# Kept rows turned by VectorE in 32x32 blocks, with the first step's h placed inside tile 6's choice

## The reference

```python
x = x + xattn(layernorm(x), ctx)          # 32 heads, 1601 keys of width 256, 8 kv heads
z = layernorm(x)
s = silu(z @ w_gate.T)                    # 1024 tokens x I = 2752
idx = top_k(-abs(s), k=I // 2)            # per token: the half of s that is smallest
s = s.at[idx].set(0)                      # is set to zero: 1376 values are kept
x = x + (s * (z @ w_up.T)) @ w_down.T
z = layernorm(x)                          # router: top 2 of 8 experts, each of rank 16
x = x + mixture(z)                        # h = z A, weighted, times B, times 8/R
```

## Time and profile before

| | |
|---|---|
| median of 3 runs | 1407.67 us (1404.67 to 1409.79) |
| profiled execution, its own time | 1406.26 us |
| its span in the trace | 1404.3 us |
| PE busy over the span | 1357.7 us (97%) |
| DVE, POOL, ACT busy | 989.0, 932.7, 740.8 us |
| DVE, ACT, POOL share | 70%, 53%, 66% |
| q1 (SP's and ACT's DMAs) | 193.68 MB, 89312 packets, 39.9% of 16 engines |

### The profile page before, as it was taken

How to read it: one execution, slowest core, us unless ns; L and a number is a source line. 1 busy time by engine, 2 the same in 40 slices (tenths; PEclk the granted TensorE clock), 3 DMA queues, 4 the chain that set the end, 5 groups by cost and what they waited for, 6 DMA issues and landing times.

```text
span 1404.3 us, 30491 instructions
## 1 busy us (share of the span) xinstructions
PE 1357.7 (97%) x12711; PEld 1007.6 (72%) x12711; DVE 989.0 (70%) x1324; ACT 740.8 (53%) x950; POOL 932.7 (66%) x627
## 2 busy tenths in 40 slices
PE   4999999999999999899999999999998999999996
PEld 3555555555555555599999998888876787887874
DVE  6888888888888888870000899999999323245655
ACT  6788888888888888742324634334241111111211
POOL 0799888888888988823344332323323899999892
PEclk9899999999999999999999999999999999999999
DMA  9023333233323230023436347557664876866552
GB/s 359 27 101 105 134 108 111 95 112 100 113 98 119 102 116 31 17 78 129 170 134 281 124 150 275 175 185 241 211 227 154 298 255 203 261 209 180 167 175 96
DMA packets 111469, 218.62 MB, mean 156 GB/s; under 512 B 8336, under 2 KB 84000, under 8 KB 106336
## 3 DMA queue, kind: packets, MB, share of 16 engines
q1 hardware_dynamic: 89312, 193.68, 39.9%
q10 hardware_dynamic: 22016, 22.96, 5.2%
HBM read 174.67 MB, written 41.94 MB: 154 GB/s over the span
## 4 chain that ended last, share of the span: by engine, by line
PE 76%; DVE 19%; DMA 1%; issue 1%; ACT 1%; SPq 0%; POOL 0%; POOLq 0%; DVEq 0%; ACTq 0%
PE fast_psum L1960 17%; PE fast_psum L2047 16%; PE fast_psum L2108 16%; PE fast_psum L1978 15%; PE fast_psum L1997 6%; DVE fast_below L1427 5%; DVE fast_near L1464 2%; DVE fast_near L1491 1%; PE fast_psum L2004 1%; DVE fast_top L1470 1%; PE fast_psum L2083 1%; DVE fast_sx L1497 1%; DMA fast_mag<-s 1%; PE fast_psum L2159 1%; PE fast_psum L1983 1%
## 5 line engine op out<-in xcount | busy, mean ns | idle before, releaser
L1357 DVE TENSOR_TENSOR fast_masked<-fast_psum,fast_mask_t 128x1024 f32<-128x1024 f32 (+1 forms) x416 | 488.4, 1219 | 72.2 <-PE fast_psum L1960 70.0
L1208 POOL TENSOR_TENSOR fast_pair<-fast_probs 128x1024 f32<-128x1024 f32 x192 | 457.1, 2384 | 96.3 <-PE fast_psum L1997 47.7
L1707 ACT ACTIVATE fast_probs<-fast_masked 128x1024 f32<-128x1024 f32 (+1 forms) x416 | 438.0, 1058 | 68.8 <-DVE fast_masked L1357 53.6
L1960 PE MATMUL fast_psum<-fast_qT,fast_kraw 32*128 32x256 f32 (+1 forms) x3328 | 247.1, 403 | 6.8 <-ACT fast_qT L1654 3.2
L1978 PE MATMUL fast_psum<-fast_probs,fast_vraw 128*32 128x256 f32 (+1 forms) x3328 | 226.5, 386 | 0.8 <-ACT fast_probs L1707 0.8
L1960 PEld LDWEIGHTS fast_psum<-fast_qT,fast_kraw 32*128 32x128 f32 (+1 forms) x3328 | 153.7, 182 | 93.3 <-DVE fast_masked L1357 53.9
L1268 POOL TENSOR_TENSOR fast_d_lo<-fast_d_raw,fast_d_hi 128x256 fp32r<-128x256 f32 x252 | 190.8, 787 | 5.0
L1241 POOL TENSOR_TENSOR fast_g_lo<-fast_g_raw,fast_g_hi 128x1408 fp32r<-128x1408 f32 x28 | 89.9, 3237 | 140.4 <-ACT fast_g_hi L1768 118.3
L2047 PE MATMUL fast_psum<-fast_g_hi,fast_z_hi 128*128 128x352 f32 x512 | 166.2, 325 | 0.0
L2047 PE MATMUL fast_psum<-fast_g_hi,fast_z_lo 128*128 128x352 f32 x512 | 165.8, 324 | 0.0
L2047 PE MATMUL fast_psum<-fast_g_lo,fast_z_hi 128*128 128x352 f32 x512 | 165.0, 322 | 0.0
(11 more groups left out here) (175 smaller groups left out, 1908.5 us busy)
## 6 DMA issues: line engine op xcount, KB each, us to landing
fast_d_raw<-w_down SPq DMA_DIRECT2D x63, 512.0 KB, 3.6
fast_kraw<-ctx_t SPq DMA_DIRECT2D x32, 800.5 KB, 6.1
fast_vraw<-ctx_nat SPq DMA_DIRECT2D x16, 1536.0 KB
fast_g_raw<-w_gate_up SPq DMA_DIRECT2D x15, 1408.0 KB, 7.3
fast_mag<-s SPq DMA_DIRECT2D x9, 1376.0 KB, 7.9
fast_u_raw<-w_up_t SPq DMA_DIRECT2D x21, 512.0 KB, 4.8
u_t<-fast_u_out SPq DMA_DIRECT2D x42, 256.0 KB, 3.2
s<-fast_res SPq DMA_DIRECT2D x14, 704.0 KB, 3.8
```

What stands on the lines that cost most here:

```text
L1208: pool.tensor_tensor(pair[:, n % PAIR_BUFS], both[:, :, 0, :], both[:, :, 1, :], ALU.add).then_inc(paired, 1)
L1357: dve.tensor_tensor(into, of, m, ALU.add).then_inc(mask_added, 1)
L1707: act.activation(probs[0:r, g % RING, hp * HALF:(hp + 1) * HALF], masked[0:r, h % SLOTS, :], ACT.Exp).then_inc(exp_done, 1)
L1960: last = pe.matmul(scores[0:r, (2 * g + hp) % SLOTS, h % 2, i * 256:(i + 1) * 256], kraw[b % BUFS][q, u, c * P:c * P + r], qT[q, b, u, :], ...
```

## The change

The kept rows are no longer stored as rows and turned by PE. `keep` writes into `near`; a new DVE instruction (`turn_kept`) transposes 32x32 blocks of the tile, from `near` to `sx`; and SP stores the result with an access pattern that puts each block's rows where they belong, so that DRAM holds `s_t`, 2752 rows of 1024 tokens. One tile goes in four pieces of 32 partitions, each 32x86x32: 2752 runs of 128 bytes. Down loads `t_s` from it as it loads `t_u`, straight into the layout of h.

With it go: `d_hi` is rounded by ACT (`round_down`) and POOL only makes `d_lo`; the choice of tiles 6 and 7 ends inside down; steps 0 and 1's multiply stand inside tile 6's choice; the third layer norm's statistics and its application are two parts, two steps apart; `xin` is loaded a tile at a time; and tables of positions move by a step or a few.

```diff
-        UP_ABS_AT = {7: 4, 12: 5, 21: 6, 26: 7}
+        UP_ABS_AT = {7: 4, 13: 5, 21: 6, 29: 7}
-        UP_SK_AT = {1: 1, 6: 2, 8: 3, 13: 4, 15: 5, 19: 6}
-        UP_SX_AT = {0: 2, 2: 3, 7: 4, 9: 5, 14: 6, 15: 7}
-        LOAD_X_AT = {0: 0, 12: 1, 30: 2}
+        PIECES_FROM = {0: 0, 4: 1, 12: 2, 16: 3, 27: 4, 31: 5}
+        UP_PIECE_AT = {i + q: (t, q) for i, t in PIECES_FROM.items() for q in range(QUARTERS)}
+        DOWN_PIECE_AT = {n + q: (t, q) for n, t in ((6, 6), (19, 7)) for q in range(QUARTERS)}
+        UP_SX_AT = {3: 2, 5: 3, 9: 4, 11: 5, 16: 6, 17: 7}
+        CHOICE_AT = {2: ("keep", 6), 4: ("turn", 6), 6: ("nearest", 7), 8: ("best", 7), 10: ("choose", 7),
+                     11: ("mark", 7), 12: ("strike", 7), 14: ("keep", 7), 16: ("turn", 7), 18: ("verdict", 7)}
+        LOAD_X_AT = {0: 0, 2: 1, 4: 2, 11: 3, 13: 4, 15: 5, 30: 6, 33: 7}
-        LN3_AT = {36: 0, 38: 1, 40: 2, 46: 3, 47: 4, 49: 5}
+        LN3_AT = {34: 0, 37: 1, 40: 2, 46: 3, 48: 4, 50: 5}
+        APPLY3_AT = {n + 2: t for n, t in LN3_AT.items()}
...
# SP
-            def store_sk(t):
-                sp.wait_ge(kept, t + 1)
...
-                sp.dma_start(sk[t * P:(t + 1) * P, :], sx[t]).then_inc(sk_stored[t % 2], 16)
+            def store_piece(t, q):
+                if q == 0:
+                    sp.wait_ge(sx_turned, t + 1)
...
+                rows_of = slice(q * BLK, (q + 1) * BLK)
+                sp.dma_start(s_t.rearrange("(b r) n -> r b n", r=BLK)[:, :, t * P + q * BLK:t * P + (q + 1) * BLK],
+                             sx[t][rows_of, :].rearrange("r (b n) -> r b n", n=BLK)).then_inc(st_stored[t % 2], 16)
...
# POOL
-                pool.wait_ge(d_full[j], 16 * loads(n, DS))
...
-                pool.tensor_copy(d_hi[j][:, :], d_raw[j][:, :]).then_inc(d_hi_done, 1)
                 pool.wait_ge(d_hi_done, n + 1)
...
# DVE
-                done(dve.scalar_tensor_tensor(sx[t], near, thr[:, :], sx[t], ALU.is_ge, ALU.mult))
+                done(dve.scalar_tensor_tensor(near, near, thr[:, :], sx[t], ALU.is_ge, ALU.mult))
...
+            def turn_kept(t):
+                dve.wait_ge(kept, t + 1)
+                dve.transpose(sx[t], near).then_inc(sx_turned, 1)
...
-                dve.tensor_tensor(t_h[n % 2][:, 0:w], bank[6 + n % 2][:, 0:w], t_u[n % TURNS][:, 0:w],
+                dve.tensor_tensor(t_h[n % 2][:, 0:w], t_s[n % TURNS][:, 0:w], t_u[n % TURNS][:, 0:w],
                                   ALU.mult).then_inc(h_ready, 1)
...
+            nearest(TILES - 2)
+            multiply(0)
+            best(TILES - 2)
+            take_low(0)
+            choose(TILES - 2)
+            mark(TILES - 2)
+            strike(TILES - 2)
+            multiply(1)
...
             for n in range(STEPS):
...
+                if n in APPLY3_AT:
+                    apply3(APPLY3_AT[n])
...
+                if n in CHOICE_AT:
+                    late_choice(*CHOICE_AT[n])
...
# ACT
+            def load_factors(n):
...
+                act.dma_start(t_s[n % TURNS][0:rows(k), 0:m * P], s_t[k * P:k * P + rows(k), t0 * P:(t0 + m) * P]
+                              ).then_inc(ts_full[n % TURNS], 16)
...
+            def round_down(n):
...
+                act.copy(d_hi[j][:, :], d_raw[j][:, :]).then_inc(d_hi_done, 1)
...
-                if i == 2 * UF - 8:
...
+                if i == 2 * UF - 5:
                     for n in range(TURNS):
-                        load_u(n)
+                        load_factors(n)
+                if i == 2 * UF - 3:
+                    round_down(0)
+                if i == 2 * UF - 2:
+                    take_high(0)
+                    round_down(1)
+            take_high(1)
...
# PE
-            def turn(n):
...
-                    last = pe.transpose(bank[6 + n % 2][:, i * P:(i + 1) * P], t_sk[q % BLOCKS][:, i, c:c + P], eye[:, :])
-                last.then_inc(t_turned, 1)
...
             for n in range(STEPS):
-                if n + 2 < STEPS:
-                    turn(n + 2)
```

More of the change, by code:

```diff
@@ L1508, in _, with late_choice @@
+            def late_choice(part, t):
+                if part == "nearest":
                     nearest(t)
+                elif part == "best":
                     best(t)
+                elif part == "choose":
                     choose(t)
-                    keep(t)
-            dve.wait_ge(step, steps[0])
-            done(dve.tensor_reduce(good[:, :], settled[:, :], AX.X, ALU.min))
-            dve.wait_ge(step, steps[0])
-            done(dve.tensor_scalar(bad[:, :], good[:, :], -1.0, 1.0, ALU.mult, ALU.add))
```

222 lines of the change are left out of this document (117 added, 105 removed).

## The result

The changed kernel takes 1390.18 us, the median of 4 runs (1388.37 to 1391.06), against 1408.35 for the kernel before, the median of 4 (1404.67 to 1409.79). The ratio is 0.9867, with a 95% interval of 0.9843 to 0.9891: it is 1.3% faster. The forecast was 1415 and slower. The profiled execution has a span of 1388.8 us, where before it was 1404.3.

A forecast was written before the change was run, and what follows sets the result against it. PE was taken to bound up and down. Gains of 32.1 us (21.7 + 9.2 + 1.2) against losses of 40.7 (19.7 + 12 + 9) gave net +8.6, from 1406.26 to about 1415, range 1384 to 1446.

The forecast's parts named there:

- The price of a piece: Queue time of one stored piece of 2752 runs of 128 bytes: 4.5 us taken, bounds 1.5 and 9.1.
- (e) to (g): Late weights and loads: up's first stretch 6.5 + 4.7 + 5.5, its second and third 12, down's tiles 6 and 7 9.
- Rival B: Pieces overlap with what is around them, losses shrink to 12, time 1387; chance 0.37.
- c: The price of a piece in us, on which the forecast result turns; 4.5 taken.
- A: The forecast itself: the queue pays, c from 4 to 5.2, net −8 to +20, time 1399 to 1428; chance 0.43.
- (a): Down without PE's transposes: 0.37 us per step, 16.3 in groups 0 and 1, 5.4 in the last; sum 21.7 gained.
- (b): Handover from up to down: 9.2 us gained if step 0's h stands ready inside tile 6's choice.
- `d_hi` on ACT costs nothing in sum: Down's cast moved to ACT, priced at 0: 1408 columns take 1.37 us, ACT busy for 10.8 of 96.0.
- (c): Tail of down: PE's wait for POOL's `d_lo`, 1.2 us, goes.
- (d): Start of up: DVE's transposes, 3.1 us each, make ACT's copy late (874.2); PE loses 2.1, taken as 3.
- rival D: A DVE transpose takes two passes, 6 us; about 6 us reach PE, time 1421; counted as part of A.
- Rival C: Short stores cost more than long ones, c of 6 or more: +55, time 1463; chance 0.20.

The follow-up runs named there:

- e4: Changed kernel with each piece in two DMAs of 2752 runs of 64 bytes, same bytes in twice the packets: 1428.87 us, ratio 1.0163.
- e2: Changed kernel with each piece stored as 32 rows of 11008 bytes, the same bytes in long runs: 1388.76 us, ratio 0.9864.
- e3: Changed kernel with each of the 32 pieces stored a second time, to another tensor: 1434.55 us, ratio 1.0197.
- e6: Changed kernel with VectorE's transposes of 128x2752 cut to 128x32, stores in the same pattern: 1384.25 us, ratio 0.9835.
- e1: Changed kernel with POOL rounding d_hi again in the last of down's groups, ACT in the first two: 1384.35 us, ratio 0.9843.
- e9: Kernel before the change with the d_hi cast of steps 0 to 33 on ScalarE instead of POOL: 1407.44 us, ratio 0.9972.
- e8: Changed kernel with the d_hi cast on POOL in all three of down's groups: 1408.13 us, ratio 0.9993.
- e7: Changed kernel with the third layer norm of tiles 0 to 5 in one part again: 1425.14 us, ratio 1.0120.
- e10: Changed kernel with the third layer norm in one part and the d_hi cast on POOL from step 34: 1390.18 us, ratio 0.9864.
- e5: Changed kernel with the first two steps' multiplies and step 0's low part behind the replace of tile 6's choice: 1390.45 us, ratio 0.9874.
- e11: e1 with ScalarE's first compares of the second pair spread over up's first five copies: 1378.75 us, ratio 0.9769.

## Why the prediction was wrong

**The price of a piece** is the step that failed. I took 4.5 us, from 251 packets in 0.4 us. That stretch is a single small load, in which the engines were busy for 69.2%; it is a start, not a rate. Filled, the queue passes a packet in 0.56 (e4) to 0.72 ns (the changed kernel). By the densest stretch a piece costs 2.0, by the queue's share in up 2.5, between the bounds of 1.5 and 9.1. I chose by likeness of packet size, where the row's own busy share said that it was no full queue. Losses (e) to (g), 6.5 + 4.7 + 5.5 + 12 + 9 = 37.7, hang on that price. Measured (e2), the short runs cost some 1.4 us in all, and the noise is as large; what would be gained with no pieces at all, no run shows. The one wait in down that could look like theirs, 0.63 us for `h_lo` at 1145, is in e2 as well: VectorE's `keep` of tile 7, 3.56 us long, stands ahead of that step's multiply.

**How losses follow from the price.** The 40.7 forecast for 4.5 us a piece look like the 44 and 39 that e3 and e4 lost, but the way there was another. The prediction let the time follow the queue's load; e4 lost 39 with the queue busy for 77.3%. Two DMAs of 2752 runs for each piece keep SP issuing for 64 to 66% of up, and without a break around tile 6's pieces in down. I had filled SP's line with the times that its DMAs take on the queue, and had no term for their issuing; each such DMA makes the next issue about 1.7 us longer.

**Rival B,** with 0.37, is what happened: its condition, c of 3.5 or less, was met, and its 1387 is 3 from the measured 1390. That it is so near is in part luck. Of the gains it took over, the last group's 5.4 didn't come and 1.3 were lost there; of its 12 of losses, e2 and e6 show 1.4 and 5.9. The two misses largely cancel. A's own numbers had a slip as well: c of 5.2 gives 8.6 + 22.4 = +31 and not +20, and the break-even is 4.2 and not 4.0. Neither changes the forecast.

**(a) Transposes, 16.3 in groups 0 and 1:** the step is 4.08, as worked out. Group 1 gained 7.4 of 8.1. Group 0 gained 4.5, and 1.8 of that is step 0 alone, 6.30 us before and 4.52 after, which the prediction had counted in (b): before, the matmuls behind the gap were slow, at a granted clock of 0.80,

```profile
1090.00:1100.00 10.00, 10.00 (x37) 8.07 (x38) 2.33 (x4) 1.03 (x2) 7.36 (x10) 0.80 1.02 351
```

and after, without the gap, it is 1.00 there. The row before has no wait for another engine; the one after has 1.85 for step 2's `d_lo`, where POOL's first part took 2.44 us beside VectorE's `keep` of tile 6, and the 0.63 at 1145. The 5.4 of the last group weren't gained: 1.3 were lost. The step that failed there is "`d_hi` on ACT costs nothing in sum": I priced the cast by ScalarE's idle time, not by what stands behind a cast that waits. It costs 5.5 us of the last group, 5.8 by the medians (e1).

**What I had at 0 and wasn't:** the cast's move carries the gain. POOL's step was 4.13 us of work with 0.31 of idle, against 4.45 on TensorE, so moving the cast alone gives nothing in the two groups (e9). With all of the change but the cast's move they take 6.7 us more than before, and the time is that of before (e8): POOL's step is then no longer 4.13, because VectorE's passes hold it up. I used POOL's limit only for the last group, and had no term for the two engines slowing each other. And the norm in two parts, also at 0, is what makes the move possible (e7, e10).

**(b) The border, 9.2:** step 1's first matmul comes 5.67 us behind up's last instead of 15.04, 9.4 less: right in size. The reason was wrong in part (e5).

**(c) The tail, 1.2:** the wait of 1377.8 is gone. It stood ahead of down's last matmul, so it is in the last group's row, which is longer all the same; from down's last matmul to the end it is 21.4 us instead of 20.8. In sum nothing was gained.

**(d) VectorE's transposes, ScalarE's late copy:** forecast 874.2 for the copy, measured 873.25, and 1.5 us of waiting for 2.1 to 3. The transpose took 3.05 for 3.1, so rival D, and with it the estimate of 6.7 us from the Trainium skill's "VectorE: DVE Perf Modes" (The three transpose paths), falls. Only up to here was the chain followed; e6 and e11 show that the same lateness, through SP's line, is nearly all that up loses against 228.3.

**Rival C,** the rule of the Trainium skill's "DMA: Bandwidth & Descriptors" (Specifications) that below 512 B there is a read-modify-write: short runs do cost more of the queue than long ones (72.4% against 62.4% in e2), but about 1.0 us a piece and not the whole price again.
